# Attention and expert pieces on one core: extra pieces moved to the middle of a slot, a shared PV bank, phases by halves of the queries, second product merged with the next turn

## The chip, the cores and the metric

One core of one Trainium2 chip runs the whole program. The metric is the device time in microseconds. Engines are named as in the profile: PE is TensorE (PEld its weight loads), DVE is VectorE, ACT is ScalarE, POOL is GpSimd, SP is the engine that issues most DMAs.

## What is computed

The input x has 4 sequences of 1024 tokens with 128 features. Two layers run one after the other, and each adds attention and a feed-forward part to x. The reference, cut to what matters:

```python
xn = _layernorm(x)
x = x + L0_attn(xn) + L0_ffn(xn)
xn = _layernorm(x)
x = x + L1_attn(xn) + L1_ffn(xn)

# L0_attn: 16 heads of 8 features, rotary positions, no mask
scores = jnp.einsum('bhqd,bhkd->bhqk', Q, K) / math.sqrt(DIM_K)
weights = jax.nn.softmax(scores, axis=-1)
out = jnp.einsum('bhqk,bhkd->bhqd', weights, V)      # then @ wo_w.T + wo_b
# L0_ffn: 8 experts, the best 2 of each token, 512 hidden features
h = jax.nn.relu(jnp.einsum('td,edf->etf', x_flat, w1) + b1[:, None, :])
y = jnp.einsum('etf,efd->etd', h, w2) + b2[:, None, :]
out = jnp.einsum('te,etd->td', combine_w, y)
# L1_attn: the same without rotation and with a causal mask
# L1_ffn: gate, up and down products of inputs rounded blockwise to FP4
h = jax.nn.silu(gate) * y
return fp4_linear(h, w_down)
```

## The kernel before

The work is cut into **slots**. A planner (`class Plan`) writes the whole order out before the program is built, and every engine walks through the same list of slots in the same order. There are eight **phases**, one for each layer and sequence, in the order `PHASES`; a phase of layer 0 has 64 slots, one of layer 1 has 48. `start` of the eight phases is slot 38, 102, 166, 214, 278, 326, 390 and 438, the last step is in slot 485, and the last slot is 491.

A slot of the steady part holds, for a group g of 4 heads:

- a **step** (`step`, kind "E"): for one tile of 128 keys (kt) and one half of 512 queries (qh), the scores of the 4 heads on PE (`scores`, two heads at a time), each into a bank of its own, then one exponential of each on ACT (`exps`, line 797) into PR;
- a **quad** (`quad`, kind "M"), 12 slots ahead of the steps: scores of 128 queries against 512 keys for the same 4 heads on PE (`maxima`), and on DVE a maximum of each (line 1140, in layer 1 on the diagonal line 1144). The row maxima, turned by an "mtr" piece, go as two more rows into QX by DMA ("rows"), so that the scores of the step come with the maximum subtracted;
- **PV** of the step of the slot before: 4 heads side by side in one bank, pO, with 9 columns of V and ones as the stationary operand, fp32. It waits for all 4 exponentials of that step (`pe.wait_ge(s_ex, 4 * (n + 1))`, line 974);
- **extra pieces** (`xs`), at most 2 or 3 a slot, placed by `put`: "fin" (turns a finished pO, which ACT copied to oT, back to tokens; DVE divides), "of" and "fp" (the turned output and its projection), "xT", "pj", "v", "lg", "rt", "cT" of the preparation of a later phase, "gu", "turn", "down", "xqT" of the layer-1 feed-forward part, and for each of 23 tiles of a sequence's expert work "gx" (turn the gathered rows), "unit" (first product; ACT applies bias and relu, 4 activations, line 866) and "y" (second product; ACT copies it to yb). PE fills a bank for each, and ACT or DVE empties it.

On PE the order in a slot is: scores of heads 0 and 1, maxima of 0 and 1, PV, scores of 2 and 3, maxima of 2 and 3, extra pieces. On ACT: exponentials 0 and 1, the copy of pO if a group ends, the copies of the preparation, exponentials 2 and 3, extra pieces. On DVE: maxima 0 and 1, small steps, maxima 2 and 3, the combination of the maxima, small steps, extra pieces, small steps.

All E, M and extra pieces go through a **ring** of 7 banks in the order in which PE makes them (`number`). Before PE fills a bank it waits until the piece 7 places before has been consumed (`vacant`). pO is the eighth bank and no part of the ring. A PE instruction's line is that of a helper: 501 for products, 504 for turns. ACT copies have line 507.

Steps and quads go by head group, then half of the queries, then keys:

```python
STEPS = [[(g, qh, kt) for g in range(NG) for qh in range(NH) for kt in range(T)],
...
```

## Time and profile before

| | |
|---|---|
| median of 3 runs | 1686.59 us (1678.15 to 1692.77) |
| the profiled execution | 1685.66 us |
| its span, first to last instruction | 1683.9 us |
| PE busy | 1501.0 us (89%) |
| DVE busy | 1350.6 us (80%) |
| ACT busy | 1153.0 us (68%) |
| mean granted TensorE clock | 0.944 |

The profiled execution lies inside the three timed runs, 0.9 us from their median, and 1.8 us of it lie around the span. PE busy counts overlapping matmuls once, but their ends are modelled, so the share says that PE is much in use and not that it never waits.

### The profile page before, as it was taken

What the parts mean: (1) busy time and instruction counts of PE and PEld (TensorE: products, weight loads), DVE (VectorE), ACT (ScalarE), POOL (GpSimd) and SP (SyncE); (2) the same over time, 40 slices, a digit from 0 to 9 for tenths busy, and PEclk for the clock granted to TensorE, in tenths of its full rate; (3) what the DMA queues carried; (4) which work ended last, traced back from release to release, by engine and by line L of the source; (5) the groups of instructions that cost most, each with busy time, mean ns of one, the idle gap of its engine ahead of it and who ended that gap; (6) DMA issues with size and microseconds to landing.
All of it is one profiled execution on the core that took longest, in us unless ns stands there. A gap on an engine that the chain in (4) does not pass through costs nothing.

```text
span 1683.9 us, 35206 instructions
## 1 busy us (share of the span) xinstructions
PE 1501.0 (89%) x10813; PEld 627.3 (37%) x10813; DVE 1350.6 (80%) x3482; ACT 1153.0 (68%) x2716; POOL 579.8 (34%) x530
## 2 busy tenths in 40 slices
PE   2688989898999999977999999999999998999996
PEld 1111334443344444422334445344444433334332
DVE  7999867679988677878889877789888888888881
ACT  1177767687888565646888856667888856666665
POOL 4012302003334362451634424231432472644440
PEclk8599989999999998989999999999999988999999
DMA  7202263333262152012531214523452100500000
GB/s 242 54 8 62 93 158 97 85 92 90 80 167 62 46 162 70 30 35 81 153 79 47 60 34 129 127 76 92 138 154 64 54 23 26 127 2 14 2 2 14
DMA packets 162918, 131.84 MB, mean 78 GB/s; under 512 B 30825, under 2 KB 130098, under 8 KB 162738
## 3 DMA queue, kind: packets, MB, share of 16 engines
q1 hardware_dynamic: 158642, 121.19, 26.2%
q0 software_dynamic: 4096, 8.40, 1.7%
q8 instruction: 94, 1.54, 0.4%
q14 instruction: 86, 0.70, 0.1%
HBM read 88.50 MB, written 40.50 MB: 77 GB/s over the span
## 4 chain that ended last, share of the span: by engine, by line
PE 59%; DVE 20%; issue 10%; ACT 6%; POOL 2%; SPq 2%; DMA 2%; DVEq 0%; ACTq 0%; POOLq 0%
PE ring L501 38%; PE pO L501 17%; DVE mparts L1140 10%; PE ring L504 4%; ACT PR L797 4%; DVE junk L1144 2%; ACT hid L866 1%; SPq L603 1%; DVE hs L1430 1%; DVE hs L1429 1%; DVE xr L1320 1%; DMA b1r<-in_b 1%; DVE am L1353 1%; DVE stats L1190 0%; DVE mparts L1144 0%
## 5 line engine op out<-in xcount | busy, mean ns | idle before, releaser
L797 ACT ACTIVATE PR<-ring 128x512 f32<-128x512 f32 (+3 forms) x1792 | 881.1, 557 | 299.0 <-PE ring L501 280.8
L1140 DVE TENSOR_REDUCE mparts<-ring 128x1 f32<-128x512 f32 x1280 | 809.1, 683 | 139.7 <-PE ring L501 124.6
L501 PE MATMUL pO<-PR,VX 128*9 128x512 f32 (+3 forms) x3584 | 446.2, 571 | 8.0 <-ACT PR L797 7.0
L501 PE MATMUL ring<-KX,QX 48*128 48x512 bf16 (+3 forms) x1792 | 338.8, 372 | 84.8 <-ACT PR L797 26.9
L501 PE MATMUL ring<-QX,KX 50*128 50x512 bf16 (+3 forms) x1792 | 337.7, 373 | 42.7 <-DVE mparts L1140 18.1
L1144 DVE CUSTOM_DVE_ANT_0 junk<-ring,diag 128x384 bf16<-128x384 f32 (+3 forms) x512 | 228.2, 487 | 68.0 <-PE ring L501 64.3
L501 PEld LDWEIGHTS ring<-QX,KX 50*128 50x128 bf16 x1792 | 89.8, 93 | 499.2 <-DVE mparts L1140 189.5
L747 POOL TENSOR_SCALAR bq<-bq 128x352 f32<-128x352 f32 (+1 forms) x40 | 47.1, 1177 | 386.7 <-ACT bq L903 386.5
L501 PEld LDWEIGHTS ring<-KX,QX 48*128 48x128 bf16 x1792 | 96.1, 95 | 187.0 <-DVE mparts L1140 47.4
L720 POOL DMA_INDIRECT rows_in<-xn,at x64 | 62.6, 978 | 269.9 <-PE pO L501 157.0
L866 ACT ACTIVATE hid<-ring,b1r 128x128 f32<-128x128 f32 x368 | 104.5, 370 | 48.4 <-PE ring L501 48.1
L501 PE MATMUL ring<-xgT,w1r 128*128 128x128 f32 x736 | 106.4, 290 | 14.7 <-DMA b1r<-in_b 13.8
L736 POOL DMA_INDIRECT ra<-rows_out,at x64 | 61.0, 953 | 148.6 <-PE pO L501 97.0
L501 PE MATMUL ring<-w2r,hid 128*128 128x128 f32 x736 | 107.1, 290 | 1.7 <-DVE mparts L1140 1.1
L501 PEld LDWEIGHTS ring<-xgT,w1r 128*128 128x128 f32 x736 | 92.7, 198 | 37.1 <-issue 29.4
L501 PEld LDWEIGHTS pO<-PR,VX 128*9 128x9 f32 x3584 | 53.4, 89 | 137.7 <-issue 107.2
L501 PEld LDWEIGHTS ring<-w2r,hid 128*128 128x128 f32 x736 | 91.0, 195 | 22.6 <-ACT PR L797 16.4
L501 PE MATMUL ring<-identb,laterb 128*128 128x128 bf16 x512 | 74.5, 228 | 0.0
L761 POOL TENSOR_SCALAR yq<-yq 128x352 f32<-128x352 f32 (+1 forms) x40 | 60.3, 1506 | 3.3
L756 POOL TENSOR_TENSOR bq<-hq,bq 128x352 f32<-128x352 f32 x64 | 59.6, 931 | 4.9
L758 POOL TENSOR_SCALAR yq<-yq 128x352 f32<-128x352 f32 (+1 forms) x40 | 60.0, 1501 | 0.0
L704 POOL TENSOR_TENSOR parts<-rb,parts 128x512 bf16<-128x512 f32 x30 | 34.7, 1156 | 68.1 <-ACT parts L507 68.1
(163 smaller groups left out, 1440.8 us busy)
## 6 DMA issues: line engine op xcount, KB each, us to landing
scratch<-parts SPq DMA_DIRECT2D x96, 256.0 KB, 3.7
w1r<-in_w SPq DMA_DIRECT2D x92, 256.0 KB
w2r<-in_w SPq DMA_DIRECT2D x92, 256.0 KB
QX<-scratch SPq DMA_DIRECT2D x128, 96.0 KB, 3.3
KX<-scratch SPq DMA_DIRECT2D x64, 192.0 KB, 3.9
xg<-rows_in SPq DMA_DIRECT2D x92, 64.0 KB
rows_out<-yb SPq DMA_DIRECT2D x92, 64.0 KB
QX<-mT SPq DMA_DIRECT2D x256, 2.0 KB
```

The lines of the kernel that those rows point to most:

```text
L501: return nc.tensor.matmul(dst, lhsT, rhs, start=start, stop=stop, **kw)
L504: return nc.tensor.transpose(dst, src, ident[0:src.shape[0], 0:src.shape[0]])
L720: nc.gpsimd.indirect_dma_start(xs[b % 2], bass.IndirectOffsetOnAxis(at[b % 2][:, c:c + 1], 0), xn[0][:, c % T, :], None).then_inc(s_sc[b], 16)
L736: nc.gpsimd.indirect_dma_start(yg[:, D * t:D * t + D], None, ys[b % 2], bass.IndirectOffsetOnAxis(at[b % 2][:, c:c + 1], 0)).then_inc(s_yg ...
L747: ins = nc.gpsimd.tensor_scalar(b_, b_, 1.0, None, ALU.max)
L756: ins = nc.gpsimd.tensor_tensor(b_, dst, b_, ALU.subtract)
L758: ins = nc.gpsimd.tensor_scalar(y, y, -1.0, 1.0, ALU.max, ALU.min)
L761: ins = nc.gpsimd.tensor_scalar(y, y, SHIFT, SHIFT, ALU.add, ALU.subtract)
L797: nc.scalar.activation(PR[:, n % 2, HALF * j + off:HALF * j + HALF], ring[plan.bank("E", k)][:, off:HALF], ACT.Exp, scale=SCALE).then_inc( ...
L866: ins = nc.scalar.activation(hid[N % 2][:, P * fc:P * fc + P], src[:, P * fc:P * fc + P], ACT.Relu, bias=b1r[N % 2][:, fc:fc + 1])
L1140: v.tensor_reduce(dst, src[:, 0:w], axis=X, op=ALU.max).then_inc(s_mr, 1)
L1144: v.tensor_tensor_reduce(out=junk[k % 2][:, 0:w], in0=src[:, 0:w], in1=diag[:, HALF - w:HALF], scale=1.0, scalar=NEG, op0=ALU.add, op1=ALU ...
```

## The change

Four things change together.

1. **Place of the extra pieces.** On PE they come directly behind PV, ahead of the scores and maxima of heads 2 and 3. On ACT they come ahead of exponentials 2 and 3, on DVE ahead of maxima 2 and 3. The ring is numbered in that order.
2. **Shared PV bank.** Two head groups, an even and the following odd one, accumulate in one pO. The stationary operand has 18 columns for each head: 9 with V and ones, 9 with zeros, the other way round for the odd group. So the copy of pO to oT and the "fin" piece come once for two groups; DVE takes one reciprocal and two products in each.
3. **Phases by halves of the queries.** Steps and quads go by half first, then by head group. The output of the first half of a phase is turned and projected in the middle of the phase. The turned output has a buffer of its own, ofT, instead of flip; otok and cT shrink to one half.
4. **Second product and turn merged.** The "gx" piece goes. A "y" piece turns the rows of the next tile and then computes the second product of its own, into the two halves of one bank, and ACT copies both with one activation. A piece ("y", p, -1) opens each sequence. A tile now takes two pieces instead of three, in slots of their own.

The diff, cut to its core:

```diff
-STEPS = [[(g, qh, kt) for g in range(NG) for qh in range(NH) for kt in range(T)],
-         [(g, qh, kt) for g in range(NG) for qh in range(NH) for kt in range(TH * (qh + 1))]]
+STEPS = [[(g, qh, kt) for qh in range(NH) for g in range(NG) for kt in range(T)],
+         [(g, qh, kt) for qh in range(NH) for g in range(NG) for kt in range(TH * (qh + 1))]]
...
-                if kt == self.kts(p, qh) - 1:
-                    self.slot(i + 1)["out"] = (p, g, qh)
-                    self.force(i + 2, ("fin", p, g, qh))
+                if g % 2 and kt == self.kts(p, qh) - 1:
+                    self.slot(i + 1)["out"] = (p, g // 2, qh)
+                    self.force(i + 2, ("fin", p, g // 2, qh))
...
         for h in range(NH):
+            i = self.start[p] + len([s for s in STEPS[layer] if s[1] <= h]) + 2
+            if layer == 0:
+                self.put(i - 12, ("cT", p, h))
             i = self.put(i, ("of", p, h))
-        for h in range(NH):
             i = self.put(i + 1, ("fp", p, h))
...
-        i = first
+        j = self.put(first, ("y", p, -1))
+        self.slot(j + 1)["sp"].append(("xs", p, 2))
         for n in range(NT):
-            i = max(i, first + n * (to - first) // NT)
-            i = self.put(i, ("gx", p, n))
...
-            j = self.put(i + 1, ("unit", p, n))
+            i = max(j + 1, first + n * (to - first) // NT)
+            j = self.put(i, ("unit", p, n))
             j = self.put(j + 1, ("y", p, n))
...
+    def pairs(self, s, pair):
+        for kind, key, n in (("E", s["step"], self.steps), ("M", s["quad"], self.quads)):
...
+            self.pairs(s, 0)
             for e in s["xs"]:
...
+            self.pairs(s, 1)
...
     VC = DK + 1
+    VW = 3 * VC
...
+        def values(p, h, kt):
+
+            g, j = h // G, h % G
+            at_ = VW * (G * (g // 2) + j) + VC * (g % 2)
+            return VX[p % 2][:, kt, at_:at_ + 2 * VC]
```

On ACT:

```diff
-                    exps(s, (2, 3))
                     for e in s["xs"]:
...
+                            dst = VX[p % 2][:, TH * h:TH * h + TH, :].rearrange("p t (m j w) -> p (t m) j w", j=G, w=VW)
+                            v4 = src[:, :].rearrange("p (u g j w) -> p u g j w", g=2, j=G, w=DK)
+                            copy(dst[:, :, :, 0:DK], v4[:, :, 0])
+                            copy(dst[:, :, :, 2 * VC:2 * VC + DK], v4[:, :, 1]).then_inc(s_freed["A"], 1)
...
-                            copy(yb[N % 2][:, :], src[:, 0:D]).then_inc(s_freed["A"], 1)
-                        if e[0] == "gx":
...
-                            copy(xgT[N % 2][:, :], src[:, 0:P]).then_inc(s_freed["A"], 1)
+                            c = slice(D if n < 0 else 0, D if n == NT - 1 else D + P)
+                            copy(yx[N % 2][:, c], src[:, c]).then_inc(s_freed["A"], 1)
...
+                    exps(s, (2, 3))
                     for e in s["late"]:
```

On PE:

```diff
-                        if kt == 0 and plan.outs[p, g, qh]:
-                            pe.wait_ge(s_oT, plan.outs[p, g, qh])
+                        first = kt == 0 and g % 2 == 0
+                        if first and plan.outs[p, g // 2, qh]:
+                            pe.wait_ge(s_oT, plan.outs[p, g // 2, qh])
                         for j in range(G):
                             h = G * g + j
-                            ins = mm(pO[OW * j:OW * j + VC, off:HALF], VX[p % 2][:, kt, VW * h:VW * h + VC],
+                            ins = mm(pO[OW * j:OW * j + 2 * VC, off:HALF], values(p, h, kt),
                                      PR[:, n % 2, HALF * j + off:HALF * j + HALF],
-                                     start=kt == 0, stop=kt == last_kt, skip_group_check=True)
+                                     start=first, stop=kt == last_kt and g % 2 == 1, skip_group_check=True)
                         ins.then_inc(s_pv, 1)
-                    scores(s, 1)
-                    maxima(s, 1)
                     for e in s["xs"]:
...
                         if e[0] == "y":
-                            N = tile(*e[1:])
-                            pe.wait_ge(*freed(("unit",) + e[1:]))
-                            for fc in range(FC):
-                                ins = mm(dst[:, 0:D], hid[N % 2][:, P * fc:P * fc + P],
-                                         w2r[N % 2][:, fc, :], start=fc == 0, stop=fc == FC - 1)
+                            N, n = tile(*e[1:]), e[2]
+                            if n + 1 < NT:
+                                pe.wait_ge(s_xg[(N + 1) % 2], 16 * ((N + 1) // 2 + 1))
+                                ins = turn(dst[:, D:D + P], xg[(N + 1) % 2][:, :])
+                            if n >= 0:
+                                pe.wait_ge(*freed(("unit",) + e[1:]))
+                                for fc in range(FC):
+                                    ins = mm(dst[:, 0:D], hid[N % 2][:, P * fc:P * fc + P],
+                                             w2r[N % 2][:, fc, :], start=fc == 0, stop=fc == FC - 1)
...
                         ins.then_inc(s_x, 1)
+                    scores(s, 1)
+                    maxima(s, 1)
```

On DVE:

```diff
-                    maxima(s, (2, 3))
-                    if s["combine"] is not None:
...
                     for e in s["xs"]:
...
                         if e[0] == "fin":
                             _, p, g, qh = e
                             o4 = src[:, :].rearrange("p (q j w) -> p q j w", j=G, w=OW)
-                            link(v.reciprocal(linv[:, :, :], o4[:, :, :, DK]))
+                            link(v.reciprocal(linv[:, :, :, :], o4[:, :, :, DK:2 * VC:VC]))
...
+                            for i in range(2):
...
+                    maxima(s, (2, 3))
+                    if s["combine"] is not None:
...
```

## Rows read from the trace of the kernel before

**Rows 1.** The page's first part: engine, busy us, share, instructions.

```profile
PE 1501.0 (89%) x10813; PEld 627.3 (37%) x10813; DVE 1350.6 (80%) x3482; ACT 1153.0 (68%) x2716; POOL 579.8 (34%) x530
```

**Rows 2.** Windows by phase: length, busy us by engine, clock, DMA share.

```profile
75.00:308.90 233.90, 202.67 (x1395) 73.39 (x1397) 189.57 (x423) 166.47 (x365) 46.80 (x45) 0.95 0.29 82
308.90:534.90 226.00, 215.03 (x1543) 89.06 (x1537) 186.82 (x405) 181.91 (x420) 61.67 (x53) 0.99 0.35 97
534.90:733.60 198.70, 182.64 (x1334) 87.58 (x1326) 146.62 (x460) 118.87 (x313) 83.76 (x78) 0.92 0.26 72
733.60:963.60 230.00, 207.65 (x1470) 80.55 (x1462) 196.79 (x443) 177.04 (x393) 91.29 (x82) 0.97 0.30 80
963.60:1137.60 174.00, 164.80 (x1271) 77.88 (x1273) 134.24 (x424) 112.61 (x296) 59.99 (x57) 0.97 0.33 89
1137.60:1366.30 228.70, 216.21 (x1585) 93.51 (x1587) 197.45 (x440) 187.30 (x437) 86.79 (x76) 0.99 0.34 94
1366.30:1534.30 168.00, 154.59 (x1132) 61.80 (x1124) 138.53 (x463) 104.62 (x251) 85.95 (x75) 0.91 0.16 42
1534.30:1642.40 108.10, 99.57 (x784) 40.48 (x788) 90.95 (x305) 69.87 (x173) 45.91 (x44) 0.95 0.03 7
```

**Rows 3.** Timeline of a layer-0 slot without extra pieces: start, us, instruction, idle before.

```profile
121.73 1.04 PE L501 MATMUL pO<-PR,VX 128*9 128x512 f32 x8
...
122.70 0.39 PE L501 MATMUL ring<-QX,KX 50*128 50x512 bf16 x2
...
123.19 2.06 ACT L797 ACTIVATE PR<-ring 128x512 f32<-128x512 f32 x4 [0.54 <-PE ring L501]
...
124.33 1.05 PE L501 MATMUL pO<-PR,VX 128*9 128x512 f32 x8
```

**Rows 4.** Timeline of PE near the end, no quads, first slot with a fin.

```profile
1655.19 1.05 PE L501 MATMUL pO<-PR,VX 128*9 128x512 f32 x8 [1.54 <-ACT PR L797]
...
1656.49 0.65 PE L504 MATMUL ring<-ident,oT 128*128 128x128 f32 x4
...
1657.79 1.05 PE L501 MATMUL pO<-PR,VX 128*9 128x512 f32 x8 [0.32 <-ACT PR L797]
...
1660.39 1.05 PE L501 MATMUL pO<-PR,VX 128*9 128x512 f32 x8 [1.01 <-ACT PR L797]
```

**Rows 5.** Timeline of a layer-0 slot with fin and unit pieces, and its end.

```profile
1232.11 0.66 PE L504 MATMUL ring<-ident,oT 128*128 128x128 f32 x4
...
1233.59 0.39 PE L501 MATMUL ring<-QX,KX 50*128 50x512 bf16 x2
...
1233.70 1.14 ACT L866 ACTIVATE hid<-ring,b1r 128x128 f32<-128x128 f32 x4 [0.56 <-PE ring L501]
...
1234.13 1.05 PE L501 MATMUL pO<-PR,VX 128*9 128x512 f32 x8
...
1234.71 2.07 ACT L797 ACTIVATE PR<-ring 128x512 f32<-128x512 f32 x4
```

**Rows 6.** Timeline of the slot before that one, with a gx piece.

```profile
1227.44 1.04 PE L501 MATMUL pO<-PR,VX 128*9 128x512 f32 x8
...
1230.27 0.39 PE L501 MATMUL ring<-KX,QX 48*128 48x512 bf16 x2 [0.67 <-ACT PR L797]
...
1230.60 1.05 PE L501 MATMUL pO<-PR,VX 128*9 128x512 f32 x8
```

**Rows 7.** Groups by form: busy us, mean ns, idle before with its releasers.

```profile
L501 PEld LDWEIGHTS pO<-PR,VX 128*9 128x9 f32 x3584 | 53.4, 89 | 137.7 <-issue 107.2 <-ACT PR L797 26.8 <-ACT xgT L507 0.2
...
L507 ACT ACTIVATE oT<-pO 128x512 f32<-128x512 f32 x64 | 38.7, 604 | 9.9 <-PE pO L501 4.8 <-remote 3.6
...
L507 ACT ACTIVATE hqT<-ring 128x256 f32<-128x256 f32 x32 | 12.5, 391 | 4.4 <-PE ring L504 4.2
...
L504 PEld LDWEIGHTS ring<-ident,mneg 128*16 128x16 f32 x64 | 5.6, 87 | 19.2 <-ACT PR L797 11.0 <-issue 5.9 <-DVE mparts L1140 1.3
```

**Rows 8.** Waits between 228 and 310 us: total, times, longest.

```profile
PE ring L501 <- DMA b1r<-in_b: 13.8, 3, 6.4
```

More of the change, by code:

```diff
@@ L189, in prepare @@
         i = self.chain("ln", i + 1, [("norm", p, t) for t in range(0, T, 2)])[-1]
-        i = max(i, flip - 1)
         for h in range(NH):
@@ L272, in number @@
                 self.combines[s["combine"]] = len(self.combines)
-            for pair in range(2):
-                for kind, key, n in (("E", s["step"], self.steps), ("M", s["quad"], self.quads)):
-                    if key is not None:
-                        for j in (2 * pair, 2 * pair + 1):
-                            k = 4 * n[key] + j
-                            self.at[kind][k] = len(self.ring)
-                            self.ring.append((kind, k))
+            self.pairs(s, 0)
             for e in s["xs"]:
@@ L299, in number @@
                     self.pools[e[1:-1]] = len(self.pools)
+    def pairs(self, s, pair):
+        for kind, key, n in (("E", s["step"], self.steps), ("M", s["quad"], self.quads)):
+            if key is not None:
+                for j in (2 * pair, 2 * pair + 1):
+                    k = 4 * n[key] + j
+                    self.at[kind][k] = len(self.ring)
+                    self.ring.append((kind, k))
     def bank(self, kind, k):
```

103 lines of the change are left out of this document (45 added, 58 removed).

## The prediction

> **What bounds the kernel now.** I read the page's first part first: PE is busy for 89% of the span, DVE for 80% [rows 1]. Neither is full, so the question is what an average slot waits for. 448 slots hold a step; I cut the trace into the phases by counting the maxima on DVE (four a slot, slots 26 to 473) and asked for windows [rows 2]. The layer-0 phases (rows one, two, four and six) take 233.9, 226.0, 230.0 and 228.7 us, 918.6 together, or 3.59 a slot, with PE busy 841.6 us, 94 to 95% in the two that carry the most expert tiles. There PE is the bound. The layer-1 phases, up to 1642.4 us, take 648.8 us for 179 slots, with PE busy 601.6 us; in their single slots DVE is often last (quantization and combination steps), as their lower clock of 0.91 and 0.92 in two of them also hints: PE pauses there.
>
> Now single slots. From the start of PV to the scores of heads 2 and 3 PE needs 122.70 - 121.73 = 0.97 us [rows 3]. Scores and maxima of two heads take 1234.13 - 1233.59 = 0.54 us [rows 5], twice a slot. PE's own work in a full slot without extras is 0.97 + 2 x 0.54 = 2.05 us. A check: the slot with fin and unit goes from PV at 1230.60 to PV at 1234.13, 3.53 us; its extras last from 1232.11 to 1233.59, 1.48 us, and 2.05 + 1.48 = 3.53 [rows 5, 6]. That slot is pure PE time.
>
> The slot without extras takes 2.60 us, not 2.05 [rows 3]. Its scores start at 122.70, ACT begins the exponentials of heads 2 and 3 0.49 us later, and PV of that step starts 1.63 us after them, because it needs all four exponentials. That this is a chain through ACT, and not DVE, is seen near the end, where no quads are left: PV follows PV at 1655.19, 1657.79 and 1660.39, again 2.60 us apart, with PE idle 0.32 and 1.01 us for ACT [rows 4]. So there is a loop PV, scores 2 and 3, exponentials 2 and 3, next PV, of 0.97 + 1.63 = 2.60 us. **What matters most is what the first of these two slots shows:** a fin of 0.65 us lies in it and the period is the same 2.60 us. At the end of a slot an extra piece lies beside exponentials 2 and 3, and its first 0.55 us (2.60 - 2.05) cost nothing.
>
> **The change, part by part.**
>
> *Extras behind PV.* They leave the shadow of exponentials 2 and 3. The loop becomes PV, extras, scores 2 and 3, exponentials 2 and 3, PV: 2.60 + X us with X the PE time of the extras. Between scores 2 and 3 and the next PV, PE then has 4 x 0.27 = 1.08 us of work against 1.63 us of ACT, in every full-width slot. What is queued behind the waiting PV on PE is everything: the next extras and the next scores, so ACT and DVE run dry behind it. The time of a layer-0 slot was max(2.60, 2.05 + X); it becomes 2.60 + X, and the sum no longer depends on how the pieces are spread. X of the four phases: PE busy 841.6 - 256 x 2.05 (524.8) = 316.8 us [rows 2]. So 256 x 2.60 + 316.8 = 982.4 us, before the other terms. The waits for landing expert weights (13.8 us between 228 and 310 us, [rows 8]) are not in this sum; I leave them out, since the tiles come at a slower pace, and keep 14 us for the range.
>
> *ACT's extras ahead of exponentials 2 and 3.* The four relu activations of a unit take 1.14 us; they start 0.11 us after the scores' start, and exponentials follow 1.12 us after it instead of 0.49 us [rows 5]. In the new order that lies in the loop: +0.63 us for each unit. Of the 92 units, 69 lay in layer-0 phases: 43 us; the other 23: 14 us. A copy of 256 columns takes 391 ns [rows 7] and starts at once, so the copy behind "y" is over when the scores arrive: 0. The other copies and tanh (0.6 us at most) add 0.1 to 0.2 us in some 60 slots; I take 0 and keep 10 us for the range. What hid the unit's activations before was the PE time of a whole slot; in the new order there is no cover.
>
> *Shared PV bank.* 32 of 64 copies of pO (604 ns, [rows 7]) and 32 of 64 fin pieces go. A fin is 0.6 us of PE, and now counts in full: 16 in layer 0, -10 us; 16 in layer 1, -10 us. The copies are hidden or save up to 0.15 us each, -5 to 0; I take 0. DVE loses 32 reciprocals, no term in PE-bound slots. V's stationary operand grows from 9 to 18 columns. Loads of 9 and of 16 columns take 89 and 87 ns [rows 7], so 0. The Trainium skill (TensorE: Matmul & The Clock Gate, "LDWEIGHTS") has the load time grow in proportion to the columns, by its formula 7.5 ns more for 9 more. For 3584 loads that would be 27 us if all were bare, an estimate from that page, and the forecast would be 1814. The rows at 9 and 16 columns speak against it.
>
> *Halves of the queries.* The counts of steps, quads, mtr and "rows" DMAs stay, and a half's maxima come as many slots ahead of its steps as before. The KX and QX loads of a phase have landed before its first quad in all phases but perhaps one (below). of, fp and cT pieces move, 0. In the tail one of, one fp and one fin piece's wait less: -2 us.
>
> *Second product and turn merged.* The turn (about 0.3 us of PE) stays, so X stays. ACT saves a separate activation, which bounds nothing. The price is that a tile needs at least two slots: 23 tiles of the first sequence, which began at slot 68 and ended at 118, end some 3 to 6 slots later. The layer-1 preparation behind them, with its stores and loads on SP's queue, moves with them, and its loads came 3 to 6 slots before the first quad. 0 to 8 us; I take 0.
>
> *Layer 1.* Half of its steps are 512 wide; narrow ones have short exponentials and no such wait. 0.55 us x 89 wide slots = 49 us, + 14 (units) - 10 (fins), on PE busy 601.6 us: 655 us against 648.8. Where DVE is last, the added waits lie beside it; so +6 us.
>
> **Sum.** Layer 0: 982.4 + 43 - 10 = 1015.4, against 918.6: +97 us. Layer 1: +6. Tail: -2. The profiled execution took 1685.66 us, within 1 us of the median, so **1685.7 + 101 = 1787 us**, 6% slower.
>
> **The rivals.**
>
> *Faster: the ring was the wait.* With one extra at a slot's end the ring has nine places, and the next slot's first maxima get the banks of scores 2 and 3. A gx slot took 3.16 us although PE had 2.05 + 0.3 us to do, with 0.67 us of PE waiting for ACT there [rows 6]. Directly behind PV the piece itself frees a bank early, and 2.60 + 0.3 = 2.90 us would do. If about 100 slots have such small pieces, that is 25 us; with 20 us of fins, 1641 us. Against it: most PE time of extras is in units, y and projections of 0.9 us and more. It decides only if PV does not wait for the exponentials just behind the extras, which rows 3 and 4 contradict. Chance 0.09.
>
> *No change.* The loop's 0.55 us falls mostly where PE already waits: the layer-0 phases contain two windows with 22 and 31 us of idle PE, and layer 1 is bound by DVE. Then fins and waits cancel: 1680 to 1700 us. Against it: PE is 94 to 95% busy in two of the four phases. Chance 0.08.
>
> *Slower by more.* DVE waits for the extra on PE in the middle of its slot, and its maxima 2 and 3 come late where it is the bound. Some 100 layer-1 slots hold an extra; at 0.3 to 0.4 us each that is 30 to 40 us. The granted clock follows PE's activity: 0.91 and 0.92 in the two layer-1 phases with PE 92% busy, 0.99 where it is 95% [rows 2]. If the added waits bring layer 0 from 0.97 or 0.99 down to 0.93, 842 us of PE work grow by 5%, 42 us, and the kernel takes 1787 + 35 + 42, about 1860 us. The Trainium skill (TensorE: Matmul & The Clock Gate, "A second HAM failure mode: psum-queue depth-cycling") describes short PE pauses between groups, from cycling through PSUM banks, that make the clock switch to and fro; by that rule this rival would be the likely one, but the phases before pause in every slot without extras and stay at 0.95 to 0.99. Chance 0.15.
>
> **How the numbers follow.** The forecast's mechanism has 0.68, with 1740 to 1830 us as its own range (half of the units' term hidden by a second piece in the slot, half of the layer-0 waits already there; above, 10 us of copies, 22 us of loads and weights and 10 us on DVE). The whole range must leave out at most 2 in 10: 1700 to 1855 us leaves out the faster case, half of the unchanged one and nearly half of the last. A measurement tells about 1% from no change. Faster by over 1%: 0.09; within 1%: 0.08; slower: 0.83.
>
> **What the profile after would show.** Right: PE's idle time for ACT's exponentials at PV and at the first maxima grows several times; a slot without extras still takes 2.60 us, one with a unit 2.60 + 1.1 + 0.6 = 4.3 us from PV to PV, one with a "y" 4.0 us; layer-0 phases of 64 slots take about 254 us; 32 copies of pO; PE's weight loads for PV still at 89 ns. Wrong: if PV follows the extras without a wait, if layer-0 phases stay at 230 us, or if units are no dearer than their PE time. The prediction fails most easily by the overlap of ACT's pieces with a second PE piece in the slot, and by the clock.

## The result, and the profile after

| | before | after |
|---|---|---|
| median of 4 runs | 1688.91 us (1678.15 to 1692.77) | 1793.88 us (1792.66 to 1796.53) |
| ratio | | 1.0635, 95% interval 1.0582 to 1.0687 |
| profiled execution | 1685.66 us | 1792.66 us |
| mean granted TensorE clock | 0.944 | 0.953 |

The change makes the kernel 105 us slower. The page's first line and the shares of the chain that ended last, after:

```profile
PE 1483.2 (83%) x10685; PEld 623.4 (35%) x10685; DVE 1347.6 (75%) x3450; ACT 1120.0 (63%) x2612; POOL 581.7 (32%) x532
...
PE 54%; DVE 19%; ACT 15%; issue 8%; POOL 2%; SPq 1%; DMA 1%; DVEq 0%; ACTq 0%
```

PE, DVE and ACT each do slightly less than before [rows 1], and each is idle more. Only ACT's share of the chain has grown, from 6% to 15%, and ACT is the emptiest of the three big engines: 63% busy. An engine that is 37% idle can still bound a loop, if its work in it can't lie beside that of the others.

The windows by phase of the changed kernel, cut as in [rows 2], one row for a phase (length, busy us by engine, clock, DMA share):

```profile
74.20:312.90 238.70, 200.47 (x1374) 73.54 (x1376) 189.59 (x420) 160.78 (x343) 47.15 (x45) 0.97 0.27 77
312.90:582.10 269.20, 219.13 (x1546) 92.50 (x1538) 183.39 (x418) 178.39 (x403) 53.85 (x46) 0.97 0.31 84
582.10:773.50 191.40, 171.21 (x1332) 84.46 (x1328) 148.30 (x442) 117.18 (x308) 99.05 (x93) 0.98 0.31 84
773.50:1017.00 243.50, 203.95 (x1451) 81.71 (x1451) 194.22 (x457) 171.54 (x378) 88.57 (x77) 1.00 0.28 71
1017.00:1200.20 183.20, 162.81 (x1262) 75.72 (x1254) 139.44 (x411) 110.44 (x286) 55.81 (x53) 0.96 0.30 84
1200.20:1466.80 266.60, 224.68 (x1571) 97.73 (x1567) 195.51 (x457) 181.17 (x412) 95.62 (x84) 0.97 0.29 79
1466.80:1643.50 176.70, 149.20 (x1098) 60.03 (x1094) 139.22 (x457) 101.11 (x248) 86.26 (x75) 0.91 0.15 39
1643.50:1749.40 105.90, 96.24 (x764) 37.58 (x768) 89.90 (x277) 65.26 (x165) 38.36 (x36) 0.95 0.03 7
```

The layer-0 phases (rows one, two, four, six) sum to 1018.0 us against 918.6, +99 us; the layer-1 phases to 657.2 against 648.8, +8. PE's busy time in the layer-0 phases is 848.2 against 841.6 us, and the clock there is the same on average (0.97, 0.97, 1.00, 0.97, against 0.95, 0.99, 0.97, 0.99). Nearly the whole difference is idle PE, most of it in the second and sixth rows, +43 and +38 us, the phases with the most expert tiles.

What ended the idle time, before (waits of the whole span: total us, times, longest) ...

```profile
PEld ring L501 <- DVE mparts L1140: 244.5, 316, 4.1
...
PEld ring L501 <- ACT PR L797: 134.3, 253, 2.2
...
ACT hid L866 <- PE ring L501: 48.1, 77, 7.5
...
PE ring L501 <- ACT PR L797: 34.5, 73, 3.3
```

... and after:

```profile
PEld ring L507 <- ACT PR L811: 183.1, 228, 1.8
PEld ring L510 <- ACT PR L811: 168.8, 195, 1.7
...
PE ring L507 <- ACT PR L811: 123.6, 228, 1.1
...
ACT hid L877 <- PE ring L507: 110.8, 89, 4.6
PEld pO L507 <- ACT PR L811: 107.9, 350, 1.6
PEld ring L507 <- DVE mparts L1152: 89.7, 133, 1.9
```

PE's matmuls now wait 123.6 us for exponentials instead of 34.5, PV's weight loads 107.9 instead of 26.8 [rows 7], while the loads' waits for maxima fell from 244.5 to 89.7 us. ACT in turn waits 110.8 instead of 48.1 us for the unit on PE: each waits for the other.

One loop of it, the timeline of a slot with a unit and of the next, with a "y" (start, us, instruction, idle before):

```profile
1225.94 1.05 PE L507 MATMUL pO<-PR,VX 128*18 128x512 f32 x8
...
1226.93 1.16 PE L507 MATMUL ring<-yx,w1r 128*128 128x128 f32 x8
...
1228.02 0.39 PE L507 MATMUL ring<-QX,KX 50*128 50x512 bf16 x2
...
1228.12 1.14 ACT L877 ACTIVATE hid<-ring,b1r 128x128 f32<-128x128 f32 x4 [1.45 <-PE ring L507]
...
1229.14 2.08 ACT L811 ACTIVATE PR<-ring 128x512 f32<-128x512 f32 x4
...
1229.90 0.39 PE L507 MATMUL ring<-KX,QX 48*128 48x512 bf16 x2 [1.05 <-ACT PR L811]
...
1230.29 1.05 PE L507 MATMUL pO<-PR,VX 128*18 128x512 f32 x8
...
1231.28 0.33 PE L510 MATMUL ring<-ident,xg 128*128 128x128 f32 x1
...
1231.44 1.06 PE L507 MATMUL ring<-w2r,hid 128*128 128x128 f32 x8
...
1232.43 0.39 PE L507 MATMUL ring<-QX,KX 50*128 50x512 bf16 x2
...
1232.54 0.38 ACT L513 ACTIVATE yx<-ring 128x256 f32<-128x256 f32 x1 [1.32 <-PE ring L507]
...
1232.91 2.06 ACT L811 ACTIVATE PR<-ring 128x512 f32<-128x512 f32 x4
...
1233.66 0.39 PE L507 MATMUL ring<-KX,QX 48*128 48x512 bf16 x2 [0.40 <-ACT PR L811]
...
1234.05 1.05 PE L507 MATMUL pO<-PR,VX 128*18 128x512 f32 x8
```

Read it as: PV 0.99 us, unit 1.09, scores, relu until 1229.14, exponentials 2 and 3, and only then the first maxima and the next PV, 4.35 us after the last. ACT had sat idle for 1.45 us before the relu. The slot with the "y" takes 3.76 us.

The rows by form that answer to [rows 7]:

```profile
L877 ACT ACTIVATE hid<-ring,b1r 128x128 f32<-128x128 f32 x368 | 105.2, 368 | 112.3 <-PE ring L507 110.8 <-issue 1.4
...
L507 PEld LDWEIGHTS pO<-PR,VX 128*18 128x18 f32 x3584 | 60.6, 96 | 129.3 <-ACT PR L811 107.9 <-issue 18.1
...
L513 ACT ACTIVATE oT<-pO 128x512 f32<-128x512 f32 x32 | 19.4, 608 | 3.1 <-PE pO L507 3.1
```

### The profile page after: what moved, and what is told of

Its sections match the earlier page's. It is cut to its first block, busy times and chain, and to the rows that moved or that the text cites. A ratio compares the mean times of both kernels' runs of the same rounds, so it can differ in the third digit from the quotient of the medians.

```text
span 1790.9 us, 34555 instructions
## 1 busy us (share of the span) xinstructions
PE 1483.2 (83%) x10685; PEld 623.4 (35%) x10685; DVE 1347.6 (75%) x3450; ACT 1120.0 (63%) x2612; POOL 581.7 (32%) x532
## 4 chain that ended last, share of the span: by engine, by line
PE 54%; DVE 19%; ACT 15%; issue 8%; POOL 2%; SPq 1%; DMA 1%; DVEq 0%; ACTq 0%
PE ring L507 30%; PE pO L507 19%; DVE mparts L1152 9%; ACT PR L811 9%; PE ring L510 4%; ACT hid L877 3%; DVE junk L1156 1%; DVE hs L1435 1%; DVE hs L1434 1%; ACT yx L513 1%; ACT th L889 1%; DVE xr L1332 1%; POOL rstd L703 1%; DVE xn L1219 1%; ACT parts L513 1%
## 5 line engine op out<-in xcount | busy, mean ns | idle before, releaser
L811 ACT ACTIVATE PR<-ring 128x512 f32<-128x512 f32 (+3 forms) x1792 | 856.5, 561 | 214.3 <-PE ring L507 206.4
L1152 DVE TENSOR_REDUCE mparts<-ring 128x1 f32<-128x512 f32 x1280 | 806.4, 683 | 177.6 <-PE ring L507 167.3
L507 PE MATMUL pO<-PR,VX 128*18 128x512 f32 (+3 forms) x3584 | 445.6, 570 | 15.6 <-ACT PR L811 11.7
L507 PE MATMUL ring<-QX,KX 50*128 50x512 bf16 (+3 forms) x1792 | 332.4, 368 | 48.3 <-DVE mparts L1152 18.4
L877 ACT ACTIVATE hid<-ring,b1r 128x128 f32<-128x128 f32 x368 | 105.2, 368 | 112.3 <-PE ring L507 110.8
L513 ACT ACTIVATE yx<-ring 128x256 f32<-128x256 f32 (+1 forms) x96 | 36.0, 375 | 136.4 <-PE ring L507 120.1
L507 PEld LDWEIGHTS ring<-yx,w1r 128*128 128x128 f32 x736 | 92.3, 197 | 57.2 <-ACT PR L811 51.9
L507 PE MATMUL ring<-yx,w1r 128*128 128x128 f32 x736 | 107.6, 291 | 0.9 <-DMA b1r<-in_b 0.9
L507 PEld LDWEIGHTS pO<-PR,VX 128*18 128x18 f32 x3584 | 60.6, 96 | 129.3 <-ACT PR L811 107.9
L507 PE MATMUL ring<-w2r,hid 128*128 128x128 f32 x736 | 98.4, 277 | 0.0
L775 POOL TENSOR_SCALAR yq<-yq 128x352 f32<-128x352 f32 (+1 forms) x40 | 60.3, 1508 | 3.3
```

The costliest lines, as they stand in the source:

```text
L507: return nc.tensor.matmul(dst, lhsT, rhs, start=start, stop=stop, **kw)
L513: return nc.scalar.activation(dst, src, ACT.Copy)
L775: ins = nc.gpsimd.tensor_scalar(y, y, SHIFT, SHIFT, ALU.add, ALU.subtract)
L811: nc.scalar.activation(PR[:, n % 2, HALF * j + off:HALF * j + HALF], ring[plan.bank("E", k)][:, off:HALF], ACT.Exp, scale=SCALE).then_inc( ...
L877: ins = nc.scalar.activation(hid[N % 2][:, P * fc:P * fc + P], src[:, P * fc:P * fc + P], ACT.Relu, bias=b1r[N % 2][:, fc:fc + 1])
L1152: v.tensor_reduce(dst, src[:, 0:w], axis=X, op=ALU.max).then_inc(s_mr, 1)
```

## The experiments

Each kernel ran beside the kernel before on the same chip; a ratio is to that, with its 95% interval. "Layer 0" and "layer 1" are the sums of the phases, cut at the maxima as above. "At the end" means in the order of before. The runs came in three groups, in which the kernel before took 1690.17 us (b_mid, a_end, a_ahead, a_relu1), 1687.85 us (a_mid2, n_merge, n_bank, a_half) and 1689.63 us (the other four). What a slot takes is counted from the start of one PV to the start of the next.

**The move alone, b_mid.** The kernel before with part 1 of the change, nothing else:

```diff
                         ins.then_inc(s_pv, 1)
-                    scores(s, 1)
-                    maxima(s, 1)
                     for e in s["xs"]:
...
+                    scores(s, 1)
+                    maxima(s, 1)
```

and the same move on ACT, on DVE and in the ring's numbering.

> The kernel before with only the place of the extra pieces changed, on PE, ACT, DVE and in the ring's numbering. If the loop PV, extras, scores 2 and 3, exponentials 2 and 3, next PV is the cause: layer 0 takes 256 x 2.60 + 317 + 43 = 1026 us instead of 919, layer 1 some 16 us more, no fins are saved, so about 1805 us (1790 to 1820), more than the changed kernel. If the shared bank, the halves or the merged piece cost the time, it stays within 1% of 1687 us.

Measured: 1852.23 us against 1690.17, ratio 1.0960 (1.0915 to 1.1006). Layer 0 takes 1019 us against 918.5, layer 1 706 against 649, the tail 51 against 41.5; the mean clock is 0.933. A unit slot takes 4.34 us from PV to PV. So the move costs the old kernel 162 us, more than the whole change costs; the rest of the change gives 58 us back: 49 in layer 1, 9 in the tail and 1 in layer 0. Layer 0 came out as reckoned, layer 1 lost 57 us where 16 was expected, and the whole lies above the expected range.

The move has a gain too. In 15 layer-0 slots a turn "gx" is the only extra. 13 of them took 2.80 to 2.95 us; in the kernel before, 11 took 2.96 to 3.16 us and none less. One of them in b_mid:

```profile
415.33 1.05 PE L504 MATMUL pO<-PR,VX 128*9 128x512 f32 x8
...
416.31 0.33 PE L507 MATMUL ring<-ident,xg 128*128 128x128 f32 x1
...
418.19 1.04 PE L504 MATMUL pO<-PR,VX 128*9 128x512 f32 x8
```

From PV to PV it is 2.86 us, the loop of 2.60 us and the turn. At the end of a slot the turn had cost 0.4 to 0.6 us more than the loop, by a wait that 2.05 + X leaves out.

**The rest alone, a_end.** The changed kernel with the extras back at the end on all engines; the edit is the reverse of the one above.

> The changed kernel with its extra pieces back at the end of the slot, all else kept. Loop theory: the added time goes, and what is left of the change is 32 fin pieces and 92 ring places fewer: about 1665 us (1650 to 1685), a little faster than before. If another part of the change costs time (tiles in at least two slots, the later preparation of the first layer-1 phase), it is 1700 us or more.

Measured: 1644.32 us (1640.99 to 1651.45), ratio 0.9739 (0.9690 to 0.9788). The windows of its first two phases ...

```profile
75.50:295.40 219.90, 199.05 (x1374) 73.00 (x1376) 188.97 (x420) 162.81 (x343) 46.91 (x45) 0.96 0.30 84
295.40:525.60 230.20, 213.37 (x1542) 90.56 (x1538) 182.55 (x417) 180.61 (x402) 53.92 (x46) 0.98 0.36 99
```

... have nearly the same work as those of the changed kernel, 19 and 39 us shorter, and in the waits of its whole span PE's and PV's for the exponentials are as small as before:

```profile
PE ring L507 <- ACT PR L811: 38.1, 85, 1.9
...
PEld pO L507 <- ACT PR L811: 29.7, 77, 1.6
```

So in the changed kernel the move costs 1793.9 - 1644.3 = 150 us, 119 in layer 0 and 32 in layer 1, and the other three parts are worth 45 us (1644.3 against 1689): 19 in layer 0, 24 in layer 1. **This version beats both kernels.** It is also 6 us below the expected range: the other three parts give more than the fins alone. By slots, 74 of the 150 us lie in the 148 slots whose extras are all emptied by ACT, 38 in the 101 whose extras are all emptied by DVE, 40 in the 95 with both.

**Extras ahead of PV, a_ahead.** If only the way from PV to scores 2 and 3 to the next PV were the loop, a piece ahead of PV would lie beside the exponentials again. PV and the copy of pO move behind the extras:

```diff
                     maxima(s, 0)
-                    if s["pv"] is not None:
...
                     for e in s["xs"]:
...
+                    if s["pv"] is not None:
...
                     scores(s, 1)
```

> The changed kernel with the extras directly ahead of PV instead of directly behind it, on ACT ahead of the copy of pO, on DVE and in the ring's numbering as in the changed kernel. Loop theory: the extras lie beside exponentials 2 and 3 again, a slot takes max(2.60, 2.05 + X) us, the relu activations lie beside PV, and the ring's own wait of small pieces at a slot's end (3.16 us with a gx piece) is gone as well: 1640 us (1615 to 1665), faster than with the extras at the end. If it is the middle place as such that costs time (DVE waits for extras between its two pairs of maxima, the ring numbered that way), it stays near 1790 us. If the ring's wait is worth nothing, it equals the version with the extras at the end.

Measured: 1794.65 us, ratio 1.0641 (1.0589 to 1.0694): nothing was won, and the theory that I sent it with fell. Layer 0 takes 1010.5 us, 8 less than in the changed kernel, layer 1 takes 5 more. The timeline of one of its unit slots:

```profile
1312.69 2.07 ACT L811 ACTIVATE PR<-ring 128x512 f32<-128x512 f32 x4 [1.49 <-PE ring L507]
...
1313.43 0.39 PE L507 MATMUL ring<-KX,QX 48*128 48x512 bf16 x2 [0.40 <-DVE mT L1414]
...
1313.83 1.16 PE L507 MATMUL ring<-yx,w1r 128*128 128x128 f32 x8
...
1314.92 1.05 PE L507 MATMUL pO<-PR,VX 128*18 128x512 f32 x8
...
1315.90 0.39 PE L507 MATMUL ring<-QX,KX 50*128 50x512 bf16 x2
```

The first maxima (1313.43) start 0.74 us after ACT has begun exponentials 2 and 3; the unit stands behind them, PV ends up 1.09 us later still, and the slot's period is 3.69 us, again 2.61 plus the whole unit. So the loop closes at the first maxima already, not at PV. The ring's numbering says why: with one extra in the slot before, the first maximum is 7 places behind that extra (whose emptying by DVE the trace names here), and the second is 7 places behind score 2 and needs the bank that exponential 2 empties. So the PE time of a unit or a "y" between the first maxima and scores 2 and 3 is bare, ahead of PV or behind it (3.69 and 3.76 us). In the changed kernel's unit slot PV starts only 0.39 us behind the first maxima, which is why both readings gave the same price there. The relu is hidden here: a unit slot takes 0.66 us less than in the changed kernel. That the kernel as a whole is no faster means that other slots lost as much; which wait did that is open.

**One activation for the unit, a_relu1.** The unit's four activations become one of 512 columns; the bias b1 is left out.

```diff
-                            for fc in range(FC):
-                                ins = nc.scalar.activation(hid[N % 2][:, P * fc:P * fc + P], src[:, P * fc:P * fc + P],
-                                                           ACT.Relu, bias=b1r[N % 2][:, fc:fc + 1])
+                            ins = nc.scalar.activation(hid[N % 2][:, :], src[:, :], ACT.Relu)
```

> The changed kernel with one relu activation of 512 columns for each unit instead of four of 128, so 0.60 us instead of 1.14 us; the bias b1 is left out. Loop theory: the activations lie bare in the loop, 92 x 0.54 = 50 us go, about 1745 us (1735 to 1755), and PV to PV in a slot with a unit falls from 4.35 to 3.8 us. If ACT's extras are hidden and only PE's time counts, it stays at 1794 us.

Measured: 1756.89 us, ratio 1.0405 (1.0361 to 1.0449), 37 us less than after. The new activation, from the rows by tile: 597 ns each.

```profile
L876 ACT ACTIVATE hid<-ring x92: 597/597/600, 171.5 to 1387.6; 128x512 f32<-128x512 f32 x92
```

The relu block falls from 1.14 to 0.60 us, by 0.54, and the median unit slot from 4.35 to 3.81 us, by 0.54. ACT's own work in front of exponentials 2 and 3 counts in full, on an engine that is 63% busy. The whole gained 37 us and not the 50 of 92 x 0.54, just outside the expected range: the full 0.54 us is shown for slots with a unit alone, of which layer 0 has 30.

**Extras between scores and maxima 2 and 3, a_mid2.** PE makes scores 2 and 3 before the extras, ACT takes exponentials 2 and 3 first, DVE stays in the changed order:

```diff
                         ins.then_inc(s_pv, 1)
+                    scores(s, 1)
                     for e in s["xs"]:
...
-                    scores(s, 1)
                     maxima(s, 1)
```

> The changed kernel with the extras one step later in the middle of the slot: behind the scores of heads 2 and 3 and ahead of their maxima; on ACT behind exponentials 2 and 3, on DVE still ahead of maxima 2 and 3. The version directly ahead of PV had shown that my loop was too short: there the extras wait as well, because the first maxima of a slot need the bank of score 2, so that whatever stands between those maxima and scores 2 and 3 of the same slot, ahead of PV or behind it, lies bare. By this corrected loop, behind scores 2 and 3 the extras lie beside the exponentials again: about 1650 us (1635 to 1675), like the version with the extras at the end. If the place between DVE's two pairs of maxima is what costs, about 1790 us, or 1700 to 1750 us if it is a part of it.

Measured in ten runs: 1686.14 us, ratio 0.9994 (0.9963 to 1.0025), above the expected 1635 to 1675. Of the 150 us of the move, 108 are gone although PE's extras still stand ahead of maxima 2 and 3. What the move did to scores 2 and 3 on PE and to their exponentials on ACT is most of the cost. The 42 us that stay, 37 in layer 0, belong to the later maxima on PE and in the ring and to DVE's order, which this run does not separate; 37 of them lie in the 196 slots with a piece that DVE empties, and none in the 148 with pieces for ACT alone.

**Less work for the exponentials, a_half.** Exponentials 2 and 3 go over half of their columns, except for the first tile of keys; the other half of those weights is left out.

```diff
-                        nc.scalar.activation(PR[:, n % 2, HALF * j + off:HALF * j + HALF],
-                                             ring[plan.bank("E", k)][:, off:HALF], ACT.Exp,
+                        lo = off if j < 2 or kt == 0 else HALF - (HALF - off) // 2
+                        nc.scalar.activation(PR[:, n % 2, HALF * j + lo:HALF * j + HALF],
+                                             ring[plan.bank("E", k)][:, lo:HALF], ACT.Exp,
```

> The changed kernel with exponentials 2 and 3 computed on half of their columns in all steps but the first of a group of keys (kt = 0), the other half left as it is; so the result is not the reference's. Each takes 0.39 us instead of 0.60. Loop theory: the loop through the bank of score 2 and the first maxima shortens by 0.22 us in each such slot, 224 slots in layer 0 and about 80 in layer 1, so about 1725 us (1700 to 1740), and a slot without extras falls from 2.60 to about 2.4 us. If ACT is not in the loop, the time stays at 1794 us, since ACT is busy for only 63%.

Measured: 1752.76 us, ratio 1.0356 (1.0294 to 1.0418), 41 us less than after. The profiled execution took 1759.5 us, 33 less than that of after, and 30 of these lie in layer 0. In single slots the theory holds in full: the median slot without extras takes 2.40 us instead of 2.61, as expected, one with a unit 4.06 instead of 4.35 and one with a "y" 3.47 instead of 3.76. The sum is 0.6 of the expected. The mean clock was 0.939 instead of 0.953, which may take back a part; which wait takes the rest is open.

**Part 4 at the end, n_merge,** a_end without the merged piece, gx, unit and y as before:

```diff
+            i = self.put(i, ("gx", p, n))
...
+            j = self.put(i + 1, ("unit", p, n))
             j = self.put(j + 1, ("y", p, n))
```

> The version with the extras at the end, without part 4: gx, unit and y are three pieces again, planned as before. It tells what the merged piece is worth there. At the end of a slot a lone gx costs 0.56 us of ring wait (3.16 us against 2.60), and 92 ring places come back: I expect 1660 us (1650 to 1670), 16 us more than the 1644 us of the version with the merged piece. If part 4 is worth nothing, 1644 us, and the gain lies in the shared bank and the halves.

Measured: 1643.19 us (1639.93 to 1645.95), ratio 0.9717 (0.9666 to 0.9769), against 1644.32 with the merge. Beside the shared bank the merge is worth nothing. It saves 9 us in the first phase (229.2 against 219.9 us) and loses as much in the others.

**Part 2 at the end, n_bank,** a_end without the shared bank:

```diff
-                if g % 2 and kt == self.kts(p, qh) - 1:
-                    self.slot(i + 1)["out"] = (p, g // 2, qh)
+                if kt == self.kts(p, qh) - 1:
+                    self.slot(i + 1)["out"] = (p, g, qh)
```

> The version with the extras at the end, without part 2: each head group has its own pO, copy and fin piece again, 64 of them; halves and merged piece stay. By the fins' PE time (0.6 us) and the ring wait of a lone fin at a slot's end (3.0 us against 2.6), 32 fins cost 12 to 20 us: 1660 us (1652 to 1668). If the copies of pO, which stand ahead of exponentials 2 and 3, count as well, 1670 us; if the gain lies in the halves, it stays at 1644 us.

Measured: 1651.43 us (1649.08 to 1656.14), ratio 0.9775 (0.9722 to 0.9828). Beside the merged piece the shared bank is worth about 7 us, at the edge of what these runs can tell.

**Part 3 alone, b_halves.** The kernel before, at its own order, with steps and quads by halves:

```diff
-STEPS = [[(g, qh, kt) for g in range(NG) for qh in range(NH) for kt in range(T)],
+STEPS = [[(g, qh, kt) for qh in range(NH) for g in range(NG) for kt in range(T)],
```

> The kernel before with part 3 alone: phases by halves of the queries, with ofT, the smaller otok and cT; own pO, copy and fin for each head group, gx, unit and y as before, extras at the end. The version with halves and merged piece ran in 1651 us, and without part 4 the one with halves and shared bank did not change. So if the halves carry the gain, which I had priced at 0: 1650 us (1643 to 1658). If it took the merged piece's slower pace of the tiles as well (it ended the weight waits of the first phase, 9 us there), 1660 us; if the halves are worth nothing by themselves, 1688 us.

Measured: 1664.73 us (1662.69 to 1674.26) against 1689.63, ratio 0.9871 (0.9833 to 0.9909). The halves alone give 25 us of the 45. It is layer 1 that gains, 615.5 us against 648.9; layer 0 loses 11. I had priced this part at nothing. With this run the prices of parts 2 and 4 turn out to hang together: from the halves alone (1664.7, ratio 0.9871) the shared bank brings 22 us (n_merge, 0.9717) and the merge 13 (n_bank, 0.9775), with intervals that do not touch, but both together bring 20 (a_end, 0.9739).

**Only DVE's order back, a_dve_old.** PE, ACT and the ring stay as changed; DVE takes maxima 2 and 3 and their combination ahead of the extras:

```diff
+                    maxima(s, (2, 3))
+                    if s["combine"] is not None:
...
                     for e in s["xs"]:
...
-                    maxima(s, (2, 3))
```

> The changed kernel with DVE's order alone as before: maxima 2 and 3 ahead of its extras; PE, ACT and the ring as in the changed kernel. The ring then makes the next slot's first maxima wait for the bank of the extra, which DVE frees 1.2 us later: if banks and not DVE's own waiting set the time, about 1 us more in each of some 100 slots where that extra stands last, 1850 us or more (1820 to 1900). If DVE's waiting between its two pairs of maxima is what costs in the changed kernel, it gets faster, 1770 us or less. If neither counts, 1794 us.

Measured: 2219.55 us, ratio 1.3131 (1.3072 to 1.3190), mean clock 0.845. In the waits of its whole span DVE waits 519.1 us for PE at the maxima of line 1152 alone (99.2 in a_end, 167.3 after):

```profile
DVE mparts L1152 <- PE ring L507: 519.1, 398, 7.9
```

The direction was expected for the case that banks set the time, the size, 426 us and not 56, was not. Slots with a unit or a "y" alone take 4.35 and 3.76 us as before this edit; 348 of the 426 us lie in the 196 slots with a piece that DVE empties.

**Only DVE's order moved, n_dve_mid.** The counterpart: a_end, with DVE's extras ahead of maxima 2 and 3.

```diff
                     for e in s["xs"]:
...
+                    maxima(s, (2, 3))
+                    if s["combine"] is not None:
```

> The version with the extras at the end on PE, ACT and in the ring, and only DVE's order as in the changed kernel: its extras ahead of maxima 2 and 3. It gives the price of DVE waiting for an extra while its maxima 2 and 3 lie ready. The version with the extras between scores 2 and 3 and maxima 2 and 3 took 42 us more than the one at the end. If DVE's order made these, about 1690 us (1675 to 1710) here too or more; if it was the later maxima on PE, 1644 to 1655 us.

Measured: 1846.03 us, ratio 1.0952 (1.0892 to 1.1012), mean clock 0.919; 202 us above a_end, far more than expected; 193 of them lie in the 196 slots with a piece that DVE empties, 3 in the 148 with pieces for ACT alone. It was meant to split the 42 us of a_mid2 and can't, since it brings a cost of its own. The timeline of a slot with y and "gu":

```profile
1342.37 0.47 PE L507 MATMUL ring<-wgT,xqT 128*128 128x176 f32 x2
...
1343.52 0.34 DVE L1434 SCALAR_TENSOR_TENSOR hs<-th,ring 128x176 f32<-128x176 f32 x1 [2.31 <-ACT th L890]
...
1344.26 2.54 DVE L1152 TENSOR_REDUCE mparts<-ring 128x1 f32<-128x512 f32 x4
...
1345.10 0.39 PE L507 MATMUL ring<-KX,QX 48*128 48x512 bf16 x2 [1.64 <-DVE mparts L1152]
...
1347.03 0.61 PE L507 MATMUL ring<-QX,KX 50*128 50x512 bf16 x2
```

DVE stands 2.31 us for the tanh of a piece that PE makes last, while the scores for maxima 2 and 3 lie finished in their banks; it takes them from 1344.26 on, and PE, waiting for the banks, starts the next maxima at 1345.10, after 1.64 us. Then two score matmuls take 0.61 us instead of 0.39: the clock has fallen, as the windows of that stretch show (columns as above):

```profile
1343.00:1345.00 2.00, 0.46 (x3) 0.10 (x2) 1.41 (x4) 1.40 (x3) 1.92 (x3) 1.00 0.13 37
...
1346.00:1347.00 1.00, 1.00 (x8) 0.00 (x0) 0.80 (x2) 0.00 (x0) 0.92 (x2) 0.50 0.89 275
```

PE was busy 0.46 of 2 us at a granted clock of 1.00, that is 2.4 GHz; two microseconds on it is 0.50, 1.2 GHz. In this kernel **the order in which banks are emptied has to be the order in which they are filled**: either mismatch costs more than the whole change. Had the change moved PE and ACT only, it would have taken 2220 us.

**Only the units back at the end, a_unit_end:**

```diff
-                    for e in s["xs"]:
+                    for e in [e for e in s["xs"] if e[0] != "unit"] + [None] + [e for e in s["xs"] if e[0] == "unit"]:
+                        if e is None:
+                            scores(s, 1)
+                            maxima(s, 1)
+                            continue
```

with the same split on ACT and in the ring's numbering.

> The changed kernel with only the unit pieces back at the end of the slot (PE, ACT and ring), all others still directly behind PV. A slot with a unit took 4.35 us in the middle order and 3.15 us with the extras at the end, so 92 x 1.15 = 106 us go if the loss adds up slot by slot: 1690 us (1680 to 1705). If the units only carry a loss that any long piece would carry, for instance through the clock or DVE, it is above 1720 us.

Measured: 1713.97 us (1713.36 to 1717.82), ratio 1.0151 (1.0125 to 1.0178). The median unit slot is at 3.15 us, as in a_end, and 80 of the 150 us of the move are gone. That is less than the 106 us of a sum slot by slot and more than the expectation's other case. Slots with a "y" stay at 3.76 us (3.43 in a_end). So somewhat over half of the move's cost is the units', by their relu block and their PE time together; the rest goes with all other pieces.

The times side by side (us). The last three columns are medians from PV to PV over layer-0 slots without extras, with a unit alone and with a "y" alone:

| kernel | time | layer 0 | layer 1 | none | unit | y |
|---|---|---|---|---|---|---|
| before | 1688.9 | 918.5 | 648.9 | 2.60 | 3.14 | 3.36 |
| after | 1793.9 | 1018.1 | 657.1 | 2.61 | 4.35 | 3.76 |
| b_mid | 1852.2 | 1019.1 | 706.2 | 2.60 | 4.34 | 3.69 |
| a_end | 1644.3 | 899.4 | 624.9 | 2.61 | 3.15 | 3.43 |
| a_ahead | 1794.7 | 1010.5 | 662.1 | 2.61 | 3.69 | 3.76 |
| a_relu1 | 1756.9 | 988.6 | 646.8 | 2.61 | 3.81 | 3.76 |
| a_mid2 | 1686.1 | 936.3 | 628.3 | 2.62 | 3.15 | 3.22 |
| a_half | 1752.8 | 987.6 | 655.9 | 2.40 | 4.06 | 3.47 |
| a_unit_end | 1714.0 | 952.2 | 643.0 | 2.61 | 3.15 | 3.76 |
| n_merge | 1643.2 | 908.2 | 616.9 | 2.61 | 3.15 | 3.36 |
| n_bank | 1651.4 | 905.2 | 627.4 | 2.60 | 3.15 | 3.43 |
| b_halves | 1664.7 | 929.4 | 615.5 | 2.60 | 3.14 | 3.37 |
| a_dve_old | 2219.6 | 1215.8 | 883.0 | 2.61 | 4.35 | 3.76 |
| n_dve_mid | 1846.0 | 1022.6 | 705.2 | 2.64 | 3.15 | 3.43 |

## Why the prediction was right, and where its parts were not

**The forecast** of 1787 us stands against 1794 us, and the mechanism it named is the one the runs show. Layer 0 was forecast at 1015.4 us and took 1018.1, layer 1 at 655 and took 657.1. That the sum came so near is in part luck, as told below.

**The loop.** A slot without extras stayed at 2.61 us, one with a unit took 4.35 (4.3 forecast), one with a "y" 3.76 (4.0 forecast: its PE time was 1.15 us, 1231.28 to 1232.43, in place of 1.4). PE's and PV's waits for the exponentials grew 3.6 and 4 times. That the loop runs through ACT is shown by a_relu1 (0.54 us off ACT, 0.54 us off the slot) and by a_half (a slot without extras at 2.40 instead of 2.61 us). The loop was drawn one step too far, though: a_ahead shows that it closes at the first maxima. For the change this made no difference, since PV and maxima start 0.39 us apart; for the next idea it did.

**The relu block.** Priced at 0.63 us for each unit; beyond the loop of 2.61 us and the unit's 1.09 us the slot took 4.35 - 3.70 = 0.65 us. Right.

**The sum of the move was too small, and the other parts too.** The prediction had for the move 982.4 + 43 - 918.6 = 107 us in layer 0, before the fins, and about 16 in layer 1; a_end shows 119 and 32. The term most mis-sized is layer 1's: the sum adds 49 + 14 us to PE's busy time of 601.6 us and so takes the 47 us that PE was idle in layer 1 before as gone ("where DVE is last, the added waits lie beside it"); 16 us are left of 63. Half of them showed in the changed kernel, and nearly all, 57 us, in b_mid. The 12 us in layer 0 are not placed by piece; a slot with a fin alone went from 3.02 us in a_end to 3.20. Against that stood the fins at 20 us, the halves and the merge at 0, when together they gave 45. Two errors of about 25 us each cancelled; taken in the other order, by b_mid, they are 39 us (162 where 123 was summed) and 36 us (58 where 22 was summed). That they cancel is luck.

**Halves at 0** was wrong: 25 us alone (b_halves), 33 won in layer 1 and 11 lost in layer 0. The count of pieces is indeed the same, which is what the price rested on. What changes is what stands beside what. The whole gain of layer 1 lies in the 90 slots with a 512-wide step, from 3.67 to 3.30 us on average; the 90 with a narrow one stayed (3.58 and 3.59). By halves, 69 of the 90 wide steps stand beside a 512-wide quad, before 51; but before, slots of both kinds took about the same (3.63 and 3.71 us), so their counts alone explain under 2 us. The extras moved as well: 1.32 in a wide slot on average, before 1.54, and 1.54 in a narrow one, before 1.33. Which of the two made the gain no run here isolated.

**Shared bank.** Forecast 20 us from fins that count in full; at the end of the slot it is 7 us beside the merged piece and 22 without it. In the middle it wasn't measured alone, but there all three other parts together gave layer 0 only 1 us (1019.1 to 1018.1), where the fins were to give 10. The load of the 18 columns took 96 ns where that of 9 took 89, and the forecast had said no growth, from the rows at 9 and 16 columns. The Trainium skill (TensorE: Matmul & The Clock Gate, "LDWEIGHTS (loading the stationary operand)") has 7.5 ns for 9 columns more. The growth agrees with that, the 89 ns themselves lie far above its formula. But the 27 us that would follow if all loads were bare did not come: from the start of PV to the next product it is 0.98 us in most slots before, and 0.98 or 0.99 after. The growth lies beside the matmuls.

**Merge at 0** was right beside the shared bank (n_merge, -1 us), though not without it (13 us). The waits for landing expert weights, kept as a doubt of 14 us, went from 13.8 to 0.9 us; those for the gathered rows (xg) went from 5.9 to 8.2. **Tail:** 41.5 us before and after, not the 2 us less of the forecast.

**The rivals.** *Faster, the ring was the wait:* for small pieces this rival named something real. A lone gx went from 2.96 to 3.16 us down to 2.80 to 2.95 with the move (b_mid), by the rival's count 2.90. The forecast's rule of max(2.60, 2.05 + X) leaves that wait out. But it is 0.15 to 0.25 us in a few slots, against 0.3 us lost with a lone "y" (3.36 to 3.69) and 1.2 us with a lone unit (3.14 to 4.34), so it did not decide. *No change:* the layer-0 phases with idle PE lost as well, 5 and 14 us (first and fourth rows), though less than the two full ones. *Slower by more, DVE and the clock:* on average the clock stayed, 0.97 to 1.00 in layer 0. That it "follows PE's activity" does not hold for all of [rows 2]: the first phase has 0.95 with PE 87% busy, the third 0.92 with 92%. Within layer 0 it did fall at times after the change too, as in the sixth row at 1318.6 us:

```profile
1314.00:1318.60 4.60, 3.25 (x23) 0.80 (x27) 4.46 (x11) 3.48 (x7) 0.00 (x0) 1.00 0.44 129
1318.60:1320.00 1.40, 1.40 (x9) 0.11 (x1) 1.36 (x4) 0.00 (x0) 0.00 (x0) 0.50 0.01 2
```

In the first of these stretches PE paused for 0.18, 0.51 and 0.65 us. The fourth row stood at 1.00 throughout, with pauses of up to 1.1 us. The Trainium skill (TensorE: Matmul & The Clock Gate, "A second HAM failure mode: psum-queue depth-cycling") describes a clock that switches to and fro behind short pauses between groups. Single falls here look like that, but they did not add up to a lower clock than before, so that rule did not decide the time. In n_dve_mid and a_dve_old, with more and longer pauses, the mean clock was 0.919 and 0.845.

## What to carry to other kernels

Ask of each place in an in-order schedule which chain of engines closes around it, and where the slack of that chain lies. A filler piece is cheap while the other engine of the loop is at work on something already handed to it. One place earlier, between a result and the work that it hands over, a long piece here was paid in full, with what its consumer does for it, whatever the engines' busy shares said. And when pieces share a ring of banks, ask whether every engine empties them in the order in which they are filled: moving the order on DVE alone, or on all but DVE, cost 202 and 426 us. Parts of a change that are priced at nothing because they only reorder should be run alone: here one was worth 25 us. Two parts that are each worth something alone may be worth little together: the shared bank brought 22 us and the merge 13, both 20. The best kernels here are the change without its first part, with the merge or without.

## What the runs showed of the hardware

- Weight loads of fp32 took 89 ns for 9 columns (PV, before), 87 for 16 (a turn, before) and 96 for 18 (PV, after). The 7 ns more on each PV load showed as at most 0.01 us from the start of PV to the next product.
- The mean granted clock of layer 0 was as high after as before, though PE paused more. Pauses alone do not tell it here: one phase with pauses of up to 1.1 us stood at 1.00, while in another the clock fell from 1.00 to 0.50 with no pause over 0.65 us in the stretch shown before it. It was 0.919 and 0.845 in the two kernels in which DVE's order differs from PE's. In the stretch shown of n_dve_mid it fell from 1.00 to 0.50 behind a pause of 1.64 us, and two score matmuls took 0.61 in place of 0.39 us.
- One relu of 512 columns takes 597 ns where four of 128 columns take 1.14 us: about 0.18 us for each activation more, (1.14 - 0.60) / 3. The single one also leaves out the bias, so a part of this may be the bias's.
